# Bias rows moved to GpSimd, expert 2 added in one late pass, and the routing moved behind the last gate

## The chip, the cores and the metric

The kernel runs on one core of one Trainium2 chip. The metric is the time of one execution in microseconds (us); lower is better. TensorE is called PE here, VectorE DVE, ScalarE ACT, GpSimd POOL and the queue that issues the DMAs SP, as in the profile.

## The reference, cut to what matters

The input x has 16 groups of 512 tokens with 128 features each. All weights are small and shared by the groups.

```python
xn  = layernorm(x)
out = x + attn(xn) + ffn(xn)
# attn: queries, keys, values of 32 features; decayed causal scores; 128 features out, times out_scale
# ffn, for every token:
logits  = xn @ router_w + router_b + load_balancer      # 4 experts
rw, sel = top_k(logits, 2); rw = softmax(rw)
e0 = silu(xn @ sw_w1) * (xn @ sw_w3) @ sw_w2            # hidden 512
e1 = gelu(three folded linear maps) @ me_c2w + me_c2b   # hidden 256
e2 = layernorm(h2 + ff(h2)) @ ce_gen_w + ce_gen_b       # h2 itself a layernorm of a linear map of xn
e3 = gelu(xn @ ml_w1 + ml_b1) @ ml_w2 + ml_b2           # hidden 512
ffn = rw[0] * stack(e0, e1, e2, e3)[sel[0]] + rw[1] * stack(e0, e1, e2, e3)[sel[1]]
```

Every expert is computed for every token. Its weight `coef[:, t, e]` is zero where the expert isn't among the two chosen.

## The kernel before

The work goes in 16 turns, one for each group of 512 tokens (four tiles `t` of 128). The function `turns` writes turns 0 and 1, then a loop whose body holds two turns (2 to 13), then turns 14 and 15 and a tail. Each engine has its own list of instructions, written out by hand in the order in which it runs them, and semaphores between them; no scheduler moves anything. A waiting instruction holds up all that stands behind it on its engine.

A turn g works on group g and on what is left of group g-1 (`g.prev()`), and gets group g+1 ready:

- PE multiplies, in this order: the token products `tok0` to `tok3` (they wait for `x_split`, the low half `xl` of the transposed input), q and k, the first gate (`a0`, `b0`), the hidden units of expert 3 (`c0` to `c3`), the transposes of the normalized tile `n1` (they wait tile by tile for `c_normed`), the scores, the second gate, experts 1 and 2 of group g-1 into the banks EX, the attention, the two `f1` units, the last two gates, `e3`, `f2`, `m0` and `m1`. Then expert 0 of group g goes into the bank that expert 2 also uses (`EX_BANK = {3: 0, 0: 1, 2: 1, 1: 0}`), so it waits for `ex_taken[2]`, and last the transposes of `u`.
- DVE builds `pl` (tokens plus logits) and its moments, the gates (`silu(j)`: L818 and L822), the low halves, the routing (ten small steps, L883 to L898 and L918, each of which waits for the one before, `route`), and mixes the experts: `mix` adds `coef * expert` to `OUT` in four instructions, one a tile (L752). Expert 2 is mixed in two passes, `expert2_scale` (L762, expert 2 times its `rstd`, plus its bias) and `expert2_add` (L771). The bias of expert 1 is added by four more (L926). Near the end of the turn stand `u` (L931), `x_low` (L706, the `xl` for which the next turn's first products wait) and `x_moments` for group g+2 (L640, L643).
- ACT takes the products out of PSUM: tanh, gelu, relu, the high halves of the split numbers, and `tlean` (L612), the tanh that turns the difference of two logits into their softmax.
- POOL runs, in every turn: `norm("c")` (L444 to L454: the root of the variance and four tiles of `n1`), `root_u`, six low halves (`hid3l`, `hidl`, L486 and L490), and `norm_x` for group g+2, which waits for `x_moments`. The next thing on its list is the next turn's `norm("c")`, which waits for `c_stats`, the moments of `pl`.
- SP carries the normalized x and the transposed expert 3 to memory and back (`swap`), loads x and stores the output (`store` waits for `out_ready`).

The order on POOL and what `norm("c")` is needed for are in these lines:

```python
# POOL, turn(g)
norm("c", pl, n1, c_normed)
...                               # root_u, hid3l, hidl
norm_x(Group(g.pair, g.off + 2))
# PE, turn(g)
pe.wait_ge(c_normed, g.count(NT, t + 1))
ins = pe.transpose(TR[:, t * P:(t + 1) * P], n1[:, t, :], ident[:, :])
# PE, expert0(g)
wait(pe, ex_taken[2], g.count(1, 0))
```

## Time and profile before

| what | value |
|---|---|
| median of 3 runs | 451.15 us (451.05 to 454.04) |
| span of the profiled execution, first to last instruction | 449.1 us |
| so outside the span, against the median | 2.05 us |
| PE busy | 438.6 us, 98% of the span |
| DVE busy | 402.5 us, 90% |
| ACT busy | 271.4 us, 60% |
| POOL busy | 245.8 us, 55% |
| from one turn to the next | 26.83 us |

The time of the profiled execution as a whole isn't listed beside its span; the medians are taken for it. A turn's length is the distance of the same instruction in two turns: the first transpose of `n1` starts at 207.64 and at 234.48 us. In a row of the timeline the first number is the start in us from the beginning of the span, the second is the duration of the piece (of all its instructions, where xN says that there are several), and a bracket at the end gives the engine's idle time before it and what ended it. Instructions of one engine overlap a little: four mixing instructions of 0.345 us take 1.05 us from the first start to the start of what follows.

### The profile page before, as it was taken

The page shows a single profiled execution, that of the slowest core. Times are in us where ns is not written, and L with a number is a line of the kernel's source. Part 1 is how long each engine was busy: PE and PEld are TensorE (multiplying, and loading weights), DVE is VectorE, ACT ScalarE, POOL GpSimd, SP SyncE. Part 2 cuts the span into 40 slices and gives each one's busy share as a digit, 9 for nine tenths or more (in the row PEclk, how much of TensorE's full clock was granted, in tenths as well). Part 3 has the DMA queues.
Part 4 walks back from the last instruction along what each step waited for, and adds up shares of the span by engine and source line. Part 5 has one row for each costly group of instructions (what it writes and reads, how often), then busy time and mean ns, then how long its engine had stood idle before and what let it go on. Part 6 is the DMA issues. An engine that isn't in the chain of part 4 may idle for free.

```text
span 449.1 us, 9603 instructions
## 1 busy us (share of the span) xinstructions
PE 438.6 (98%) x2804; PEld 371.8 (83%) x2804; DVE 402.5 (90%) x1344; ACT 271.4 (60%) x535; POOL 245.8 (55%) x366
## 2 busy tenths in 40 slices
PE   4999999999999999999999999999999999999997
PEld 3778888788888888888888988888888888888886
DVE  4887989989899898989989899898989989898897
ACT  4965838557384764838556484755838566483841
POOL 3893727557273664727466272664727466372451
PEclk9999999999999999999999999999999999999999
DMA  7522123032130412223032130413123031220201
GB/s 261 38 72 72 25 63 78 26 93 47 51 70 23 105 35 70 47 70 70 23 93 47 55 62 23 113 27 89 27 70 70 23 99 41 58 58 16 58 0 48
DMA packets 86484, 27.18 MB, mean 61 GB/s; under 512 B 64993, under 2 KB 82113, under 8 KB 86465
## 3 DMA queue, kind: packets, MB, share of 16 engines
q1 hardware_dynamic: 86176, 26.94, 25.0%
q8 instruction: 9, 0.15, 0.1%
q14 instruction: 11, 0.08, 0.1%
q10 hardware_dynamic: 288, 0.01, 0.0%
HBM read 14.66 MB, written 12.06 MB: 60 GB/s over the span
## 4 chain that ended last, share of the span: by engine, by line
PE 94%; DVE 3%; DMA 1%; issue 0%; DVEq 0%; ACT 0%; SPq 0%
PE S L1133 14%; PE S L1135 13%; PE S L1134 13%; PE EX L1059 12%; PE EX L1079 6%; PE S L1223 3%; PE S L1218 3%; PE S L1219 3%; PE EX L1087 3%; PE TR L1173 2%; PE S L1231 2%; PE S L1230 2%; PE S L1229 2%; PE S L1148 2%; PE S L1147 2%; PE S L1146 2%
## 5 line engine op out<-in xcount | busy, mean ns | idle before, releaser
L486 POOL TENSOR_TENSOR hid3l<-hid,hid3h 128x512 fp32r<-128x512 f32 x64 | 80.3, 1287 | 29.3 <-ACT hid3h L599 29.3
L1133 PE MATMUL S<-xh,WH 128*128 128x512 f32 x224 | 90.4, 403 | 0.0
L1135 PE MATMUL S<-xh,WL 128*128 128x512 f32 x224 | 88.4, 394 | 0.0
L1134 PE MATMUL S<-xl,WH 128*128 128x512 f32 x224 | 88.1, 393 | 0.0
L444 POOL TENSOR_TENSOR veps_x<-mv_x,eps 128x4 f32<-128x4 f32 x16 | 3.2, 200 | 111.7 <-DVE mv_x L643 111.7
L1059 PEld LDWEIGHTS EX<-scaled,hid 128*128 128x128 f32 x480 | 55.9, 192 | 1.2
L1059 PE MATMUL EX<-scaled,hid 128*128 128x128 f32 x480 | 56.0, 275 | 0.0
L1133 PEld LDWEIGHTS S<-xh,WH 128*128 128x128 f32 x224 | 42.2, 188 | 14.1 <-DVE hid L822 3.1
L1135 PEld LDWEIGHTS S<-xh,WL 128*128 128x128 f32 x224 | 42.1, 188 | 9.9
L573 ACT COPY kv<-S 128x64 f32<-128x64 f32 x64 | 13.6, 213 | 60.3 <-PE S L1148 54.6
L1134 PEld LDWEIGHTS S<-xl,WH 128*128 128x128 f32 x224 | 42.3, 189 | 8.0
L822 DVE TENSOR_TENSOR hid<-gate,S 128x512 f32<-128x512 f32 x64 | 44.0, 688 | 4.2
L490 POOL TENSOR_TENSOR hidl<-hid,hidh 128x512 fp32r<-128x512 f32 x32 | 40.9, 1300 | 11.0 <-ACT hidh L609 11.0
L818 DVE SCALAR_TENSOR_TENSOR gate<-th,S 128x512 f32<-128x512 f32 x64 | 43.8, 684 | 1.8
L567 ACT ACTIVATE th<-S 128x512 f32<-128x512 f32 x64 | 38.1, 595 | 8.8 <-PE S L1135 6.9
L588 ACT ACTIVATE hid<-S,VEC 128x512 f32<-128x512 f32 x64 | 38.8, 690 | 0.4
L752 DVE SCALAR_TENSOR_TENSOR OUT<-EX,coef,OUT 128x128 f32<-128x128 f32 x124 | 34.8, 344 | 0.6 <-PE EX L1069 0.2
L599 ACT CAST hid3h<-hid 128x512 fp32r<-128x512 f32 x64 | 34.6, 615 | 0.0
L621 ACT ACTIVATE hid<-S,me_b 128x512 f32<-128x512 f32 x32 | 22.0, 687 | 19.2 <-PE S L1135 19.1
L519 ACT CAST xh<-TR 128x512 fp32r<-128x512 f32 x16 | 9.4, 588 | 37.6 <-DVE TR L800 37.4
L1079 PEld LDWEIGHTS EX<-W,hid 128*128 128x128 f32 x240 | 29.1, 191 | 1.3
L454 POOL TENSOR_SCALAR n<-pl,negmean_c,rstd_c 128x128 f32<-128x128 f32 x64 | 27.8, 451 | 2.8 <-issue 2.8
(201 smaller groups left out, 1066.4 us busy)
## 6 DMA issues: line engine op xcount, KB each, us to landing
X<-x SPq DMA_DIRECT2D x16, 256.0 KB, 2.8
turning<-xn SPq DMA_DIRECT2D x15, 256.0 KB, 2.6
xb<-turning SPq DMA_DIRECT2D x60, 64.0 KB, 2.6
turning<-e3T SPq DMA_DIRECT2D x15, 256.0 KB, 2.4
e3b<-turning SPq DMA_DIRECT2D x60, 64.0 KB, 2.6
out<-OUT SPq DMA_DIRECT2D x15, 256.0 KB, 2.4
W<-weights SPq DMA_DIRECT2D x1, 768.0 KB, 8.2
W<-weights SPq DMA_DIRECT2D x1, 512.0 KB, 5.8
```

Source lines behind the costliest of these rows:

```text
L486: pool.tensor_tensor(hid3l[:, j, :], hid[3][:, j, :], hid3h[:, j, :], ALU.subtract) \
L490: pool.tensor_tensor(hidl[:, j, :], hid[2][:, j, :], hidh[:, j, :], ALU.subtract) \
L567: act.activation(th[:, j, :], a[:, :], ACT.Tanh, scale=0.5).then_inc(th_ready, 1)
L588: act.activation(hid[3][:, j, :], c[:, :], ACT.Gelu, bias=vec(f"ml_b1{j}")).then_inc(free, 1)
L752: ins = dve.scalar_tensor_tensor(out=OUT[g.par][:, t, :], in0=(src or EX[EX_BANK[e]])[:, t, :], scalar=coef[g.par][:, t, e:e + 1], in1=OUT ...
L818: dve.scalar_tensor_tensor(out=gate[:, j, :], in0=th[:, j, :], scalar=1.0, in1=a[:, :], op0=ALU.add, op1=ALU.mult).then_inc(a_free, 1)
L822: dve.tensor_tensor(hid[0][:, j, :], gate[:, j, :], b[:, :], ALU.mult).then_inc(b_free, 1)
L1059: ins = pe.matmul(EX[EX_BANK[0]][:, t, :], hid[0][:, j, t * P:(t + 1) * P], scaled[:, j * P:(j + 1) * P], start=(j == 0), stop=(j == 3))
L1079: ins = pe.matmul(EX[EX_BANK[1]][:, t, :], hid[1][:, j, t * P:(t + 1) * P], w("me_c2w", j * P, P), start=(j == 0), stop=(j == 1))
L1133: pe.matmul(bank[:, :], wh, hi, start=True, stop=False)
L1134: pe.matmul(bank[:, :], wh, lo, start=False, stop=False)
L1135: pe.matmul(bank[:, :], wl, hi, start=False, stop=True).then_inc(unit_ready, 1)
```

## The change

- The bias of expert 1 (`me_c2b`) and the bias of expert 2 (`gen_bias`) are multiplied with their weights and added to `OUT` by POOL: a new function `add_biases(g)` with four instructions on 128x512 elements and two drains. It waits for `att_added` and for the last step of the routing of group g, and stands between `hidl` and `norm_x`. DVE's four instructions of L926 go.
- Expert 2 of group g-1 is mixed by one pass `expert2` of four instructions straight from its PSUM bank, with `coef * rstd` as the factor, behind the routing. `expert2_scale` and `expert2_add` go.
- The routing's first nine counted steps move from behind the second gate to behind the last gate and `turn_next`, and their scratch from PSUM (`TR`) to SBUF. ACT's `tlean` moves behind `e3T`.
- DVE takes the first gate before the low half of q.
- The turn's end: `coef` now comes before the transpose `e3t`; `store` waits for the mixing of expert 3, which is the last one; the tail loses the four instructions of L949, and `mix(g, 3, ...)` of the last group waits for POOL's sum.

```diff
             # POOL, turn
                     pool.tensor_tensor(hidl[:, j, :], hid[2][:, j, :], hidh[:, j, :], ALU.subtract) \
                         .then_inc(hid_low, 1)
+                add_biases(g, first)
                 if two_more(g):
                     norm_x(Group(g.pair, g.off + 2))
+
+            def add_biases(g, first):
+                if first:
+                    pool.wait_ge(bias_rows_loaded, 2 * DMA_INC)
+                    pool.wait_ge(setup_took, TAKEN.index("gen_b") + 1)
+                pool.wait_ge(att_added, g.count(1, 1))
+                pool.wait_ge(route_step, g.count(ROUTE_STEPS, ROUTE_STEPS))
+                wide = [P, NT, P]
+                pool.tensor_tensor(bias1[:, :, :], row("me_c2b").unsqueeze(1).broadcast_to(wide),
+                                   coef[g.par][:, :, 1:2].broadcast_to(wide), ALU.mult)
+                pool.tensor_tensor(bias2[:, :, :], gen_bias[:, :].unsqueeze(1).broadcast_to(wide),
+                                   coef[g.par][:, :, 2:3].broadcast_to(wide), ALU.mult)
+                pool.drain()
+                pool.tensor_tensor(bias1[:, :, :], bias1[:, :, :], bias2[:, :, :], ALU.add)
+                pool.drain()
+                ins = pool.tensor_tensor(OUT[g.par][:, :, :], OUT[g.par][:, :, :], bias1[:, :, :], ALU.add)
+                ins.then_inc(biases_added, 1)
             # ACT, turn
-                act.wait_ge(lean_ready, g.count(1, 1))
-                act.activation(tlean[:, :, :], lean[:, :, :], ACT.Tanh).then_inc(tlean_ready, 1)
                 half_gate(3)
...
+                act.wait_ge(lean_ready, g.count(1, 1))
+                act.activation(tlean[:, :, :], lean[:, :, :], ACT.Tanh).then_inc(tlean_ready, 1)
                 for j in range(2):
                     m, free = unit(f"m{j}")
             # DVE
-            def expert2_scale(g):
-            def expert2_add(g):
+            def expert2(g):
                 dve.wait_ge(u_rstd, g.count(1, 1))
+                dve.tensor_tensor(coef_r[:, :], coef[g.par][:, :, 2], rstd["u"][:, :], ALU.mult).then_inc(u_scaled, 1)
+                dve.wait_ge(u_scaled, g.count(1, 1))
                 dve.wait_ge(ex_ready[2], g.count(1, 1))
+                dve.wait_ge(ex_taken[1], g.count(1, 1))
+                for t in range(NT):
+                    ins = dve.scalar_tensor_tensor(out=OUT[g.par][:, t, :], in0=EX[EX_BANK[2]][:, t, :],
+                                                   scalar=coef_r[:, t:t + 1], in1=OUT[g.par][:, t, :],
+                                                   op0=ALU.mult, op1=ALU.add)
                 ins.then_inc(ex_taken[2], 1)
...
-                dve.wait_ge(qk_high, g.count(2, 1))
-                dve.tensor_tensor(Q[C:2 * C, :], qk_bank[C:2 * C, :], Q[C:2 * C, :], ALU.subtract)
                 silu(0)
                 if not first:
                     u_combine(g.prev())
+                dve.wait_ge(qk_high, g.count(2, 1))
+                dve.tensor_tensor(Q[C:2 * C, :], qk_bank[C:2 * C, :], Q[C:2 * C, :], ALU.subtract)
...
                 silu(3)
                 if not first and not last:
                     turn_next(g)
+                route(...)        # nine counted steps and lean, as before, scratch in SBUF
+                if first:
+                    turn_next(g)
+                if not first:
+                    expert2(g.prev())
+                dve.wait_ge(tlean_ready, g.count(1, 1))
+                route(...)        # coef
                 if not first:
                     ...           # e3t
-                    mix(g.prev(), 3, ex_taken[1], src=e3t)
+                    mix(g.prev(), 3, ex_taken[2], src=e3t)
```

On POOL, in the loop's body, from the last two low halves of a turn to `norm_x`, the kernel before has these rows, in which `hidl` is the low half for `f2` and `xn` the normalized x of the group after next:

```order
L490 TENSOR_TENSOR hidl<-hid,hidh 128x512 [waits hid_high]
L490 TENSOR_TENSOR hidl<-hid,hidh 128x512
L458 REGISTER_ALU
L444 TENSOR_TENSOR veps_x<-mv_x,eps 128x4 [waits x_stats]
L445 TENSOR_TENSOR negmean_x<-mv_x,minus 128x4
L447 TENSOR_TENSOR rstd_x<-veps_x,nhalf 128x4
L454 TENSOR_SCALAR xn<-X,negmean_x,rstd_x 128x128 x4
L477 REGISTER_ALU
L444 TENSOR_TENSOR veps_c<-mv_c,eps 128x4 [waits c_stats]
L445 TENSOR_TENSOR negmean_c<-mv_c,minus 128x4
L447 TENSOR_TENSOR rstd_c<-veps_c,nhalf 128x4
L454 TENSOR_SCALAR n<-pl,negmean_c,rstd_c 128x128 x4
```

The changed kernel has these in the same place:

```order
L492 TENSOR_TENSOR hidl<-hid,hidh 128x512 [waits hid_high]
L492 TENSOR_TENSOR hidl<-hid,hidh 128x512
L504 ISA [waits att_added]
L506 TENSOR_TENSOR bias<-ROW,coef 128x512 [waits route_step]
L508 TENSOR_TENSOR bias<-gen_bias,coef 128x512
L511 TENSOR_TENSOR bias<-bias 128x512
L513 TENSOR_TENSOR OUT<-OUT,bias 128x512
L460 REGISTER_ALU
L446 TENSOR_TENSOR veps_x<-mv_x,eps 128x4 [waits x_stats]
L447 TENSOR_TENSOR negmean_x<-mv_x,minus 128x4
L449 TENSOR_TENSOR rstd_x<-veps_x,nhalf 128x4
L456 TENSOR_SCALAR xn<-X,negmean_x,rstd_x 128x128 x4
```

Four tensor instructions of the full width and their wait for `route_step` now stand ahead of `norm_x`, and so also ahead of the next turn's `norm("c")`.

On DVE, in the loop's body, from the transpose of expert 3 (`e3t`) to `xl`, the kernel before has these rows, in which `u` is the input of expert 2's last product and `xl` the low half of the next group:

```order
L915 STREAM_TRANSPOSE e3t<-e3b 128x512 [waits e3_swapped,ex_taken3]
L918 SCALAR_TENSOR_TENSOR coef<-tlean,half 128x16 [waits tlean_ready]
L830 REGISTER_ALU
L752 SCALAR_TENSOR_TENSOR OUT<-e3t,coef,OUT 128x128 [waits ex_taken1,ex_ready3,route_step]
L752 SCALAR_TENSOR_TENSOR OUT<-e3t,coef,OUT 128x128 x3
L926 SCALAR_TENSOR_TENSOR OUT<-ROW,coef,OUT 128x128 [waits att_added]
L926 SCALAR_TENSOR_TENSOR OUT<-ROW,coef,OUT 128x128 x3
L805 REGISTER_ALU
L931 SCALAR_TENSOR_TENSOR u<-S,VEC,h 128x512 [waits unit_ready]
L705 REGISTER_ALU
L706 TENSOR_TENSOR xl<-TR,xh 128x512 [waits x_high]
```

In the changed kernel, behind the ten rows of the routing that now follow `TR<-xb`, stand these:

```order
L786 SCALAR_TENSOR_TENSOR OUT<-EX,coef_r,OUT 128x128 [waits ex_taken1,ex_ready2,u_scaled]
L786 SCALAR_TENSOR_TENSOR OUT<-EX,coef_r,OUT 128x128 x3
L924 SCALAR_TENSOR_TENSOR coef<-tlean,half 128x16 [waits tlean_ready]
L844 REGISTER_ALU
L130 REGISTER_ALU [waits route_step]
L929 STREAM_TRANSPOSE e3t<-e3b 128x512 [waits e3_swapped,ex_taken3]
L773 SCALAR_TENSOR_TENSOR OUT<-e3t,coef,OUT 128x128 [waits ex_taken2,ex_ready3]
L773 SCALAR_TENSOR_TENSOR OUT<-e3t,coef,OUT 128x128 x3
L819 REGISTER_ALU
L934 SCALAR_TENSOR_TENSOR u<-S,VEC,h 128x512 [waits unit_ready]
L726 REGISTER_ALU
L727 TENSOR_TENSOR xl<-TR,xh 128x512 [waits x_high]
```

`expert2` now reads the bank of expert 2 here and not some 8 us earlier, `coef` stands behind it, and the routing, `expert2` and `coef` all stand ahead of `u` and `xl`; the four rows of L926 and the four of L771 are gone.

## Rows read from the trace of the kernel before

**Rows 1.** The page: busy time of PE to POOL, granted clock, chain by engine.

```profile
PE 438.6 (98%) x2804; PEld 371.8 (83%) x2804; DVE 402.5 (90%) x1344; ACT 271.4 (60%) x535; POOL 245.8 (55%) x366
...
PEclk9999999999999999999999999999999999999999
...
PE 94%; DVE 3%; DMA 1%; issue 0%; DVEq 0%; ACT 0%; SPq 0%
```

**Rows 2.** Timeline of POOL, turn 7 and start of turn 8.

```profile
211.14 5.03 POOL L486 TENSOR_TENSOR hid3l<-hid,hid3h 128x512 fp32r<-128x512 f32 x4 [1.96 <-ACT hid3h L599]
...
227.25 0.20 POOL L444 TENSOR_TENSOR veps_x<-mv_x,eps 128x4 f32<-128x4 f32 x1 [7.83 <-DVE mv_x L643]
...
228.93 1.74 POOL L454 TENSOR_SCALAR xn<-X,negmean_x,rstd_x 128x128 f32<-128x128 f32 x4 [0.17 <-issue]
231.29 0.20 POOL L444 TENSOR_TENSOR veps_c<-mv_c,eps 128x4 f32<-128x4 f32 x1 [0.63 <-DVE mv_c L853]
...
232.96 1.74 POOL L454 TENSOR_SCALAR n<-pl,negmean_c,rstd_c 128x128 f32<-128x128 f32 x4 [0.18 <-issue]
```

**Rows 3.** Timeline of PE, turn 8: the transposes of `n1`.

```profile
234.48 0.65 PE L1173 MATMUL TR<-ident,n 128*128 128x128 f32 x4
```

**Rows 4.** Timeline of PE's weight loads, end of turn 7: expert 0, `u`, first token product.

```profile
223.68 3.77 PEld L1059 LDWEIGHTS EX<-scaled,hid 128*128 128x128 f32 x32
227.36 0.47 PEld L1246 LDWEIGHTS ATT<-ident,u 128*128 128x128 f32 x4
227.80 0.19 PEld L1146 LDWEIGHTS S<-TH,xh 128*128 128x128 f32 x1
```

**Rows 5.** Timeline of DVE, turn 7: first routing step, `foundl`, what follows the routing.

```profile
213.06 0.17 DVE L883 COPY TR<-pl 128x16 f32<-128x16 f32 x1
...
214.31 0.29 DVE L716 TENSOR_TENSOR foundl<-ATT,foundh 128x128 fp32r<-128x128 f32 x1
...
215.50 1.13 DVE L762 SCALAR_TENSOR_TENSOR e<-EX,rstd_u,gen_bias 128x128 f32<-128x128 f32 x4
```

**Rows 6.** Timeline of DVE, turn 7: from the last gate to the moments of x.

```profile
219.43 0.69 DVE L822 TENSOR_TENSOR hid<-gate,S 128x512 f32<-128x512 f32 x1
...
220.67 0.67 DVE L915 STREAM_TRANSPOSE e3t<-e3b 128x512 f32<-128x512 f32 x1
221.26 0.13 DVE L918 SCALAR_TENSOR_TENSOR coef<-tlean,half 128x16 f32<-128x16 f32 x1
221.44 1.14 DVE L752 SCALAR_TENSOR_TENSOR OUT<-e3t,coef,OUT 128x128 f32<-128x128 f32 x4
...
223.55 0.74 DVE L931 SCALAR_TENSOR_TENSOR u<-S,VEC,h 128x512 f32<-128x512 f32 x1
224.21 0.68 DVE L706 TENSOR_TENSOR xl<-TR,xh 128x512 fp32r<-128x512 f32 x1
...
225.85 0.87 DVE L640 BATCH_NORM_STATS2 stats_x<-X 128x6 f32<-128x128 f32 x4
```

**Rows 7.** Timeline of POOL, start: the low halves of the weights, one by one.

```profile
11.69 2.36 POOL L471 TENSOR_TENSOR WL<-W,WH 128x1024 fp32r<-128x1024 f32 x1 [1.72 <-DVE xn L696]
...
14.01 2.29 POOL L471 TENSOR_TENSOR WL<-W,WH 128x768 fp32r<-128x768 f32 x1
```

**Rows 8.** DVE: timeline at the start, and the tile `h2l` (min/median/max ns).

```profile
13.33 1.27 DVE L710 TENSOR_TENSOR backl<-back,backh 128x512 fp32r<-128x512 f32 x1
...
L875 DVE TENSOR_TENSOR h2l<-h,h2h x16: 678/693/694, 23.1 to 424.8; 128x512 fp32r<-128x512 f32 x16
```

**Rows 9.** POOL: the tile `rstd_u` (min/median/max ns, first and last start).

```profile
L500 POOL TENSOR_TENSOR rstd_u<-veps_u,nhalf x16: 1006/1007/1188, 47.2 to 442.6; 128x4 f32<-128x4 f32 x16
```

**Rows 10.** Timeline of DVE, end of turn 15.

```profile
437.83 0.74 DVE L931 SCALAR_TENSOR_TENSOR u<-S,VEC,h 128x512 f32<-128x512 f32 x1
```

**Rows 11.** Timeline of PE, end of turn 15: the transposes of `u`.

```profile
438.69 0.60 PE L1246 MATMUL ATT<-ident,u 128*128 128x128 f32 x4
```

**Rows 12.** Waits: engine and line, for whom; us in total, times, longest.

```profile
PEld S L1133 <- DVE gate L818: 3.1, 15, 0.2
```

More of the change, by code:

```diff
@@ L202, in build @@
         rstd = {k: sb(f"rstd_{k}", [P, NT]) for k in "xcu"}
-        more = sb("more", [P, NT, E, E])
+        same, more = (sb(name, [P, NT, E, E]) for name in ("same", "more"))
+        again, rank, top = (sb(name, [P, NT, E]) for name in ("again", "rank", "top"))
+        topsum = sb("topsum", [P, NT])
         lean = sb("lean", [P, NT, E])
@@ L832, in turn @@
                 logit = pl[:, :, P:P + E]
[L833 to L837 removed]
+                mine = again[:, :, :].unsqueeze(3).broadcast_to([P, NT, E, E])
                 other = logit.unsqueeze(2).broadcast_to([P, NT, E, E])
@@ L911, in turn @@
                     turn_next(g)
+                route(dve.tensor_copy(again[:, :, :], logit))
+                route(dve.tensor_tensor(same[:, :, :, :], other, mine, ALU.is_equal))
+                route(dve.tensor_tensor(same[:, :, :, :], same[:, :, :, :],
+                                        earlier[:, :, :].unsqueeze(1).broadcast_to([P, NT, E, E]), ALU.mult))
+                route(dve.tensor_tensor(more[:, :, :, :], other, mine, ALU.is_gt))
+                route(dve.tensor_tensor(same[:, :, :, :], more[:, :, :, :], same[:, :, :, :], ALU.add))
+                route(dve.tensor_reduce(rank[:, :, :], same[:, :, :, :], AX.X, ALU.add))
+                route(dve.scalar_tensor_tensor(out=top[:, :, :], in0=rank[:, :, :], scalar=1.5, in1=logit,
+                                               op0=ALU.is_lt, op1=ALU.mult))
+                route(dve.tensor_reduce(topsum[:, :], top[:, :, :], AX.X, ALU.add))
+                dve.scalar_tensor_tensor(out=lean[:, :, :], in0=topsum[:, :].unsqueeze(2).broadcast_to([P, NT, E]),
+                                         scalar=-0.5, in1=logit, op0=ALU.mult, op1=ALU.add).then_inc(lean_ready, 1)
+                route(dve.tensor_scalar(half[:, :, :], rank[:, :, :], 1.5, 0.5, ALU.is_lt, ALU.mult))
+                if first:
[3 more added lines that the diff above has]
+                dve.wait_ge(tlean_ready, g.count(1, 1))
+                route(dve.scalar_tensor_tensor(out=coef[g.par][:, :, :], in0=tlean[:, :, :], scalar=1.0,
+                                               in1=half[:, :, :], op0=ALU.add, op1=ALU.mult))
                 if not first:
@@ L916, in turn @@
                         .then_inc(ex_ready[3], 1)
-                dve.wait_ge(tlean_ready, g.count(1, 1))
-                route(dve.scalar_tensor_tensor(out=coef[g.par][:, :, :], in0=tlean[:, :, :], scalar=1.0,
-                                               in1=half[:, :, :], op0=ALU.add, op1=ALU.mult))
-                if first:
-                    turn_next(g)
-                if not first:
-                    mix(g.prev(), 3, ex_taken[1], src=e3t)
-                dve.wait_ge(att_added, g.count(1, 1))
-                for t in range(NT):
-                    ins = dve.scalar_tensor_tensor(out=OUT[g.par][:, t, :], in0=row("me_c2b"),
-                                                   scalar=coef[g.par][:, t, 1:2], in1=OUT[g.par][:, t, :],
-                                                   op0=ALU.mult, op1=ALU.add)
-                ins.then_inc(bias1_added, 1)
+                if not first:
+                    mix(g.prev(), 3, ex_taken[2], src=e3t)
                 f2, free = unit("f2")
@@ L934, in turn @@
                     x_low(g.next())
-                if not first:
-                    expert2_add(g.prev())
                 if two_more(g):
```

63 lines of the change are left out of this document (13 added, 50 removed).

## The prediction

> **What bounds the kernel now.** Start with the page [rows 1]: PE is busy for 98% of the span and the chain that ended last runs through PE for 94% of it. PE has no idle time to give back, so nothing that is taken off DVE or POOL shortens a turn unless PE waits for it. The question is therefore only what PE waits for, now and afterwards. Next come the timelines of one turn of 26.83 us, here from turn 7 to turn 8, engine by engine. Read in each the last moment at which PE needs something. There are four such moments: the first weight load of expert 0 at 223.68, that of `u`'s transposes at 227.36, that of the token products at 227.80 [rows 4], and the fourth transpose of `n1`, which starts some 0.4 us behind the first, so near 234.87 (four in 0.65 us [rows 3]). Then read when the other engines deliver. DVE has `u` by 224.21 and `xl` by 224.89 [rows 6], 3 us early. POOL is the tight one. It idles for 7.83 us until the moments of x arrive, runs `norm_x` from 227.25 to 230.67 (3.42 us), waits 0.63 us more, and runs `norm("c")` from 231.29 to 234.70 [rows 2]. PE's fourth transpose comes 0.17 us after that. So POOL's 55% of busy time hides that its last step ahead of PE has hardly any slack: whatever starts `norm("c")` later by more than some 0.1 us is paid by PE in every turn.
>
> **The change part by part**, in the clock of turn 7. Up to the last gate DVE is paced by PE and ACT, so the last gate still ends at 219.43 + 0.69 = 220.12 [rows 6]. The time that the routing leaves free behind the second gate turns into idle time.
>
> *Routing, later.* In the old place it took from 213.06 to 215.50, less some 0.24 for the `foundl` in its midst: 2.2 us for ten steps, 0.22 each [rows 5]. Scratch in SBUF may save a little of it; I take 2.2. It starts where the transpose of expert 3 stood, at 220.67 [rows 6], and ends at 222.87.
>
> *Expert 2 in one pass.* The factor and its wait cost about one routing step, 0.25, then four mixing instructions cost 1.05 (from 221.44 to 223.55 DVE did eight, 2.11 [rows 6]). It ends at 224.2. PE wants its bank at 223.68 [rows 4]: a wait of 0.6 us that wasn't there.
>
> *Coef* is 0.18 (221.26 to 221.44 [rows 6]), so POOL can start at 224.37. Before, DVE had `coef` at 221.4.
>
> *The biases on POOL.* POOL has run 128x512 subtractions four at a time in 5.03, so 1.26 each [rows 2]. Four make 5.0, two drains of about 0.17 (the idle in front of `xn` [rows 2] follows one) make it 5.35. The broadcast operands are not in the trace; I bound an instruction by 1.18 (2.36 for 1024 elements) and 1.53 us (2.29 for 768 [rows 7]), and take 1.26, the row of the same size. Without any disturbance the biases end at 229.72, `norm_x` at 233.14, and `norm("c")` starts at 233.17 in place of 231.29: 1.9 us late, and PE with it. DVE's eight saved instructions (L926 and one of expert 2's passes, 2.1 us a turn) buy nothing, as DVE wasn't what PE waited for.
>
> *POOL and DVE at the same time.* In a turn of before, DVE's mixing of expert 3 (both inputs in SBUF) runs while POOL idles. Now it falls into the bias instructions. The start of the trace shows what that costs. `backl`, a DVE subtraction of two SBUF tensors, took 1.27 us, the same form as `h2l` only 0.69 [rows 8]. It began at 13.33 while POOL's instruction ran from 11.69 to 14.05, and it ended at 14.60, that is 0.55 after POOL's end. POOL's next one started at 14.01 and took 2.29 for 768 elements, while 1024 took 2.36 [rows 7]: it seems to have waited for `backl`. So the two took turns, and each waited for the whole of the other's instruction. In the tail POOL's `rstd_u`, 1.007 us as a rule, took 1.188 at 442.6 [rows 9], where DVE ran four such mixing instructions in a row: it waited for one of them, not for all four. I take it that POOL gets in between DVE's instructions, and DVE between POOL's.
>
> Then: the first bias instruction runs from 224.37 to 225.63, and the first mixing instruction waits for its end. The second bias instruction gets in next, 225.75 to 227.0. Behind it POOL drains, and two mixing instructions pass. The third runs 227.35 to 228.6, then the last mixing instruction. So `u` starts at 228.85 in place of 223.55, `xl` ends 1.34 later, at 230.2. PE's token products wait for it: 2.45 late. The moments of x start at 230.1 and take 1.3, `norm_x` starts at 231.5 and takes 3.42, `norm("c")` starts at 234.9 in place of 231.29: 3.6 late. That is the turn's price, since the waits before it are inside it and the rest of the turn hangs on PE from there.
>
> *The Trainium skill* bears on this. Its page "SBUF — State Buffer", section "Who interferes with whom", says that DVE and GpSimd share one pair of ports under an exclusive lock, that a DVE instruction with two SBUF inputs contends with a GpSimd instruction that reads SBUF, and that the second to issue is blocked until the first has finished. By that rule the mixing of expert 3 is blocked here, while the plain sum gives 1.9 us a turn and not 3.6. `backl` agrees (1.27 against 0.69 us [rows 8]). That page gives no order for two queues of such instructions.
>
> *The first gate ahead of q's low half* frees its banks earlier. PE's weight loads waited there for 3.1 us over 15 turns [rows 12], for each of the gate's two instructions. They run ahead of the products, so at most that comes back, and now PE stands waiting a little later for `norm("c")` anyway: nothing.
>
> *Store, tlean.* `store` is 3 us later, with DMAs needed again only 20 us later; `tlean` runs at 222.8 beside expert 2's pass: nothing.
>
> *The tail.* In turn 15 `u` is late by the same 5.3 us (437.83 in before [rows 10]), PE had 0.2 us to spare (438.69 [rows 11]), and all that ends the kernel hangs on it: 5.1 us. The four removed instructions of L949 don't help, since the last mixing of expert 3 waits for the biases too.
>
> *Sum.* Fourteen boundaries between turns (0 to 14) have `norm_x` in them: 14 x 3.6 = 50.4. The boundary from 14 to 15 has none, there `xl` decides: 2.4. Tail: 5.1. Together 57.9, on the span of 449.1, or on the median of 451.15: **509 us**.
>
> **The rivals.**
>
> *The biases and DVE don't disturb each other.* Then a turn costs 1.9, the last boundary 0.6 (expert 2's bank), the tail 4.2 (the biases' end): 26.6 + 4.8 = 31.4, so 482.5 us. `backl` speaks against it.
>
> *DVE keeps the ports for its four instructions in a row.* One wait only; mixing ends at 226.7, POOL's biases at 230.75, `norm("c")` starts 2.9 late: 40.6 + 0.6 + 5.2, so 497.5 us. The `rstd_u` row speaks against it.
>
> *Strict turns, one for one.* The drains don't let a second one pass; mixing ends at 230.25, `xl` at 231.6, `norm("c")` starts 5.05 late: 70.7 + 3.9 + 6.6, so 532 us.
>
> *Only expert 2's bank is paid.* If POOL's four instructions took under 3.5 us, 15 x 0.6 = 9: 460 us. Nothing in rows 2 supports that.
>
> *Not slower.* POOL's idle 7.83 us covers the biases and DVE's saved 2.1 us pulls everything forward. The mechanism is DVE's lighter end of turn: it decides if the biases are done by the time the moments of x are, that is if `coef` plus the biases end by 227.3, 3.0 us after `coef` and not 5.35, and expert 2's pass ends by 223.7. Then only PE's waits at the first gate go, of which at most 3.1 us come back [rows 12]; with a third of that, 450 us. The idle time speaks for it; it lies before 224.4, though, and not behind.
>
> *The clock.* It was granted at full level throughout [rows 1]. PE would now stand still for some 2.4 and then 1.2 us a turn; if that took it to the lower level, the time would go beyond 532.
>
> **How the numbers follow.** 509: 0.36. Strict turns, 532: 0.16. One wait, 497.5: 0.15. No disturbance, 482.5: 0.16. Bank only, 460: 0.05. Not slower, 450: 0.05. Clock or worse: 0.07. The range 482 to 533 leaves out the last three, 0.17, and takes in the bounds of the bias instruction (4 x 0.27 x 15 = 16 us up, 5 down). A measurement of this kernel tells about 1%. Faster by more: 0.02; within it: 0.04; slower by more: 0.94.
>
> **What would show it.** A turn of some 30.4 us; PE idle before the transposes of `n1` with POOL's n1 named, and before the token products or `u`'s transposes with DVE named; the mixing of expert 3 from `e3t` with a mean well above 0.35 us; POOL's idle before `veps_c` gone; DVE idle before L897 and L832. I am wrong if PE's first wait is at expert 0's load alone, if the mixing keeps its 0.345 us, or if the bias instructions take far from 1.26 us.

## The result and the profile after

The changed kernel takes **501.91 us** (median of 4 runs, 500.80 to 502.95) where the kernel before, run beside it, took 451.78 (4 runs): 1.1115 times as long, 95% interval 1.1082 to 1.1147. The execution in the trace took 502.95 us with a span of 501.2, against 449.1 before, so 52.1 us are to be found. The page, whose lines answer to [rows 1]:

```profile
PE 462.1 (92%) x2804; PEld 381.9 (76%) x2804; DVE 402.7 (80%) x1231; ACT 272.6 (54%) x535; POOL 321.4 (64%) x430
...
PEclk9999899999999999999999999999999999999998
...
POOL 34%; issue 27%; POOLq 16%; PE 11%; DVE 8%; ACT 2%; DMA 1%; DVEq 0%; SPq 0%
```

PE has fallen from 98% to 92% of a longer span, and the chain that ended last, once 94% PE, goes through POOL and its queue. DVE's busy time is the same as before (402.7 against 402.5) although it has 113 instructions fewer. The groups of instructions say why (line, engine, operation, busy us and mean ns of one, idle time before):

```profile
L506 POOL TENSOR_TENSOR bias<-ROW,coef 128x512 f32<-128x512 f32 x16 | 16.8, 1048 | 78.8 <-DVE coef L924 78.8
...
L773 DVE SCALAR_TENSOR_TENSOR OUT<-e3t,coef,OUT 128x128 f32<-128x128 f32 x60 | 45.7, 819 | 0.5
...
L773 DVE SCALAR_TENSOR_TENSOR OUT<-EX,coef,OUT 128x128 f32<-128x128 f32 x124 | 34.9, 344 | 3.8 <-PE EX L1075 1.5
```

The same instruction of the same line takes 344 ns when its source is EX, in PSUM, and 819 when it is `e3t`, in SBUF. What PE waited for (us in total, times, longest):

```profile
PEld ATT L1241 <- DVE u L934: 18.5, 15, 4.7
...
PEld ATT L1150 <- DVE stats_u L801: 9.9, 13, 1.2
PEld EX L1055 <- DVE OUT L786: 9.0, 14, 1.0
PEld TR L1168 <- POOL n L456: 6.6, 19, 2.0
```

A steady turn, from the timeline of POOL, to be laid beside [rows 2]; the last gate's second instruction on DVE starts at 244.61:

```profile
249.52 1.05 POOL L506 TENSOR_TENSOR bias<-ROW,coef 128x512 f32<-128x512 f32 x1 [4.92 <-DVE coef L924]
250.53 1.09 POOL L508 TENSOR_TENSOR bias<-gen_bias,coef 128x512 f32<-128x512 f32 x1
...
255.88 0.20 POOL L446 TENSOR_TENSOR veps_x<-mv_x,eps 128x4 f32<-128x4 f32 x1 [1.31 <-DVE mv_x L664]
...
259.27 0.20 POOL L446 TENSOR_TENSOR veps_c<-mv_c,eps 128x4 f32<-128x4 f32 x1
```

And DVE's, beside [rows 6]:

```profile
244.61 0.69 DVE L836 TENSOR_TENSOR hid<-gate,S 128x512 f32<-128x512 f32 x1
...
249.28 0.17 DVE L924 SCALAR_TENSOR_TENSOR coef<-tlean,half 128x16 f32<-128x16 f32 x1
...
250.22 3.09 DVE L773 SCALAR_TENSOR_TENSOR OUT<-e3t,coef,OUT 128x128 f32<-128x128 f32 x4
253.24 0.74 DVE L934 SCALAR_TENSOR_TENSOR u<-S,VEC,h 128x512 f32<-128x512 f32 x1
```

Coef starts 4.67 us after that gate instruction starts (before: 221.26 less 219.43, 1.83). The four mixing instructions take 3.09 in place of 1.14. Even so POOL, done with the biases, stands 1.31 us waiting for the moments of x; `norm_x` starts late because DVE is late, and `norm("c")` starts right behind it (14.66 us after the gate instruction, 11.86 before). That is 2.80 us, and it is the turn: expert 0's first weight load comes every 29.6 us (101.20 to 397.42 in ten turns), before every 26.83.

Where the 52.1 us are, from those loads: 3.7 in the first turn, of which 3.0 stand ahead of its first gate (20.63 us, before 17.66); 5.1 at the boundary from turn 0 to 1; 36.4 in thirteen boundaries of 2.8; 6.9 from there to the end. The first turn varies by up to 3 us from one profiled execution to another (first load at 39.53 here, at 37.38 in e3 and at 36.38 in e1 below, whose first turns are the same code up to there), so I compare turns wherever I can.

### The profile page after: what moved, and what is told of

The parts are those of the page before. It is cut to its first block, busy times and chain, and to the rows that moved or that the text cites. A ratio compares the mean times of both kernels' runs of the same rounds, so it can differ in the third digit from the quotient of the medians.

```text
span 501.2 us, 9588 instructions
## 1 busy us (share of the span) xinstructions
PE 462.1 (92%) x2804; PEld 381.9 (76%) x2804; DVE 402.7 (80%) x1231; ACT 272.6 (54%) x535; POOL 321.4 (64%) x430
## 3 DMA queue, kind: packets, MB, share of 16 engines
HBM read 14.66 MB, written 12.06 MB: 53 GB/s over the span
## 4 chain that ended last, share of the span: by engine, by line
POOL 34%; issue 27%; POOLq 16%; PE 11%; DVE 8%; ACT 2%; DMA 1%; DVEq 0%; SPq 0%
POOL hid3l L488 10%; POOL hidl L492 6%; POOLq L454 6%; POOLq L512 4%; POOL n L456 4%; POOL OUT L513 4%; POOL xn L456 3%; POOLq L510 3%; POOL bias L508 3%; POOL rstd_u L521 2%; POOLq L448 2%; DVE gate L832 1%; DVE OUT L773 1%; POOLq L520 1%; PE EX L1075 1%
## 5 line engine op out<-in xcount | busy, mean ns | idle before, releaser
L506 POOL TENSOR_TENSOR bias<-ROW,coef 128x512 f32<-128x512 f32 x16 | 16.8, 1048 | 78.8 <-DVE coef L924 78.8
L1055 PEld LDWEIGHTS EX<-scaled,hid 128*128 128x128 f32 x480 | 54.8, 192 | 9.1 <-DVE OUT L786 9.0
L832 DVE SCALAR_TENSOR_TENSOR gate<-th,S 128x512 f32<-128x512 f32 x64 | 43.8, 684 | 20.8 <-ACT th L588 20.8
L1055 PE MATMUL EX<-scaled,hid 128*128 128x128 f32 x480 | 57.5, 278 | 2.9 <-DVE OUT L786 2.9
L773 DVE SCALAR_TENSOR_TENSOR OUT<-e3t,coef,OUT 128x128 f32<-128x128 f32 x60 | 45.7, 819 | 0.5
L897 DVE TENSOR_TENSOR OUT<-ATT,X 128x512 f32<-128x512 f32 x16 | 11.1, 692 | 27.3 <-PE ATT L1204 27.3
```

The source lines that it names most:

```text
L773: ins = dve.scalar_tensor_tensor(out=OUT[g.par][:, t, :], in0=(src or EX[EX_BANK[e]])[:, t, :], scalar=coef[g.par][:, t, e:e + 1], in1=OUT ...
L832: dve.scalar_tensor_tensor(out=gate[:, j, :], in0=th[:, j, :], scalar=1.0, in1=a[:, :], op0=ALU.add, op1=ALU.mult).then_inc(a_free, 1)
L1055: ins = pe.matmul(EX[EX_BANK[0]][:, t, :], hid[0][:, j, t * P:(t + 1) * P], scaled[:, j * P:(j + 1) * P], start=(j == 0), stop=(j == 3))
```

## The experiments

Turns are the distance between expert 0's first weight loads, averaged over nine or more turns. The kernel before has 26.83 us, the changed one 29.62.

**e1. The changed kernel without the bias work.** Left out are the four wide instructions and the drains; the bias rows are never added.

```diff
-                pool.tensor_tensor(bias1..., row("me_c2b")..., coef[...1:2]..., ALU.mult)
...
-                ins = pool.tensor_tensor(OUT[g.par]..., OUT[g.par]..., bias1..., ALU.add)
+                ins = pool.tensor_tensor(touched[:, :], eps4[:, :], eps4[:, :], ALU.add)
```

> The changed kernel with the four wide bias instructions and their drains on GpSimd left out (the bias rows are never added; a 128x4 addition waits and signals in their place), all else as in the changed kernel: late routing, one late pass of expert 2. My theory, that the 2.8 us a turn come from GpSimd's bias work (its 5.1 us in front of norm("x"), and the blocking of the mixing of expert 3), expects a turn of 26.8 to 27.4 us and 455 to 463 us, the rest being the turns 0 and 15 and PE's wait for expert 2's bank. The rival, that the late routing (2.2 us between the last gate and x_moments) carries the loss by itself, expects about 2 us a turn kept, 480 us or more.

Measured: 467.22 us, ratio 1.037 [1.0334, 1.0407], turn 27.77. The mixing from `e3t` is back at 1.14 us for four. So the bias work costs 1.85 us a turn in this surrounding, and 0.94 is there without it, more than I had allowed. PE pays 0.6 of it in every turn before expert 2's bank, and the rest in some turns before `stats_u` (five waits, 1.7 us together), in the others before `n1`. A turn of the first kind:

```profile
230.97 3.65 PEld L1048 LDWEIGHTS EX<-scaled,hid 128*128 128x128 f32 x32 [0.61 <-DVE OUT L779]
...
236.69 0.19 PEld L1143 LDWEIGHTS ATT<-xh,WH 128*128 128x128 f32 x1 [0.29 <-DVE stats_u L794]
```

**e2. POOL just as busy, but reading nothing.** Memsets of nearly the same length; the bias rows are never added.

```diff
-                pool.tensor_tensor(bias1..., row("me_c2b")..., coef[...1:2]..., ALU.mult)
+                pool.memset(filler[:, 0:1116], 0.0)
...
-                ins = pool.tensor_tensor(OUT[g.par]..., OUT[g.par]..., bias1..., ALU.add)
+                pool.memset(filler[:, 0:1300], 0.0)
```

> The changed kernel with the four bias instructions replaced by memsets of about the same length (1116, 1116, 1349 and 1300 elements a partition by the rate of the two memsets of the setup rows, 0.84 ns an element, and two 128x4 additions, 4.9 us together) that write SBUF and read nothing; the bias rows are never added. If GpSimd's reads of SBUF block VectorE's two-SBUF-source mixing, the mixing is free here and only the queue in front of norm("x") stays: GpSimd would be done near 254.6 where norm("x") started at 255.9 in the changed kernel, so 1.3 us a turn come back and 1.5 stay: 480 to 486 us, the mixing instructions at 0.35 us. If the loss were the occupation of GpSimd alone, with no blocking, nothing comes back: 499 to 503 us.

Measured: 478.36 us, ratio 1.062 [1.0571, 1.067], turn 28.1, just under my range. POOL of e2:

```profile
238.59 1.03 POOL L507 MEMSET filler<- 128x1116 f32 x1
239.55 1.03 POOL L508 MEMSET filler<- 128x1116 f32 x1
240.70 1.22 POOL L510 MEMSET filler<- 128x1349 f32 x1
242.04 1.18 POOL L512 MEMSET filler<- 128x1300 f32 x1
243.34 0.20 POOL L447 TENSOR_TENSOR veps_x<-mv_x,eps 128x4 f32<-128x4 f32 x1
```

The mixing from `e3t` takes 348 ns on average, beside memsets of nearly the same length. The wait for `mv_x` is gone, and POOL's queue alone decides. Of the 1.85 us of the bias work, 0.35 is its place in POOL's queue, and 1.5 is that it reads SBUF while DVE mixes from SBUF. The Trainium skill has this distinction ("SBUF — State Buffer", section "SBUF: two separate sides"): a DVE instruction with two SBUF inputs needs the shared ports only against a GpSimd instruction that reads SBUF. The trace agrees: 348 ns beside memsets, 819 beside the bias instructions.

**e3. Expert 3 mixed behind the moments of x.** In every turn but the last:

```diff
-                if not first:
+                if last:
                     wait(dve, ex_taken[3], g.prev().count(1, 0))
                     ... (transpose e3t, mix expert 3)
...
                 if two_more(g):
                     x_moments(Group(g.pair, g.off + 2))
+                if not first and not last:
+                    ... (transpose e3t, mix expert 3)
```

> The changed kernel with expert 3's transpose and its mixing moved behind u, x_low and x_moments in every turn but the last (nothing left out). The bias work and its contention stay, but the moments of x no longer stand behind the blocked mixing. Blocking theory: mv_x is there before GpSimd has done the biases, norm("x") starts when they end, 1.3 us earlier than in the changed kernel: 28.3 us a turn, 480 to 487 us. Rival, that GpSimd's queue alone decides when norm("x") starts: no gain, 500 us or more.

Measured: 484.34 us, ratio 1.0713 [1.0675, 1.0751], turn 28.4. The biases stay as they were and 1.2 us a turn come back from DVE's order alone. Blocking costs where the blocked instruction stands ahead of what sets the turn. Here that is POOL's queue: from the first bias instruction (240.21) to the end of `norm("c")` (252.19) POOL waits for no other engine. The mixing is still blocked (mean 621 ns), and PE waits 0.97 us in most turns for `stats_u`, which now stands right behind it; but `mv_c` is there before POOL gets to it, so that this wait doesn't lengthen the turn.

**e4. The routing back in its old place.** Its scratch stays in SBUF.

```diff
                 if first:
                     found_rest(g)
+                route(dve.tensor_copy(again[:, :, :], logit))
+                ... (the routing, as in the changed kernel)
-                route(dve.tensor_copy(again[:, :, :], logit))
-                ... (the same lines, behind the last gate)
```

> The changed kernel with the routing instructions (VectorE) and the tanh (ScalarE) back in their old places, their scratch still in SBUF; biases on GpSimd and the single pass of expert 2 stay. The coefficients are ready 2.2 us earlier after the last gate, and the bias work and the blocked mixing begin that much earlier. I expect norm("c") 12.5 us after the last gate (14.66 in the changed kernel, 11.86 before), so about 0.6 us a turn of the 2.8 stay: 455 to 465 us. Rival, that the blocked mixing costs the same wherever the routing stands: 27.5 us a turn or more, at least 480 us.

Measured: **520.07 us**, ratio 1.1529 [1.1505, 1.1554], turn 30.7. Both of my readings missed: it is slower than the changed kernel, and not through the mixing, which takes its 3.1 us as there. In the timeline of DVE, beside [rows 5]:

```profile
246.66 0.38 DVE L893 COPY again<-pl 128x16 f32<-128x16 f32 x1
247.07 1.26 DVE L894 TENSOR_TENSOR same<-pl,again 128x64 f32<-128x64 f32 x1
248.37 1.20 DVE L895 TENSOR_TENSOR same<-same,earlier 128x64 f32<-128x64 f32 x1
249.59 0.22 DVE L897 TENSOR_TENSOR more<-pl,again 128x64 f32<-128x64 f32 x1
...
250.57 1.27 DVE L903 SCALAR_TENSOR_TENSOR top<-rank,pl 128x16 f32<-128x16 f32 x1
251.87 0.17 DVE L905 TENSOR_REDUCE topsum<-top 128x4 f32<-128x16 f32 x1
252.07 1.01 DVE L906 SCALAR_TENSOR_TENSOR lean<-topsum,pl 128x16 f32<-128x16 f32 x1
```

The POOL rows of the same stretch:

```profile
244.50 4.98 POOL L488 TENSOR_TENSOR hid3l<-hid,hid3h 128x512 fp32r<-128x512 f32 x4 [1.62 <-ACT hid3h L620]
250.52 2.53 POOL L492 TENSOR_TENSOR hidl<-hid,hidh 128x512 fp32r<-128x512 f32 x2 [1.04 <-ACT hidh L630]
```

An instruction on 64 elements takes 1.26 us in place of 0.23. Each one that has both operands in SBUF ends when one of POOL's six subtractions ends (248.3, 249.5, 251.8, 253.05); `more`, which falls in POOL's pause from 249.5 to 250.5, takes 0.22; `topsum`, a reduction with one source, runs through beside `hidl` in 0.17. The routing takes 6.5 us in place of 2.4. In the kernel before the scratch was TR, in PSUM, so only one operand came from SBUF. The two edits of the routing belong together: with its scratch in SBUF it can't stand where POOL subtracts.

**e5. e4 with the scratch in PSUM.**

```diff
+                same = TR[:, 0:NT * E * E].rearrange(...)
+                again, rank, top = (TR[:, (E + n) * NT * E:...] for n in range(3))
```

> The changed kernel with routing and tanh in their old places and the routing's scratch in TR, a PSUM bank, as before; biases on GpSimd and the late single pass of expert 2 stay. It differs from e4_route_early in the place of the scratch (and one found_rest step). New theory, read in the trace of e4_route_early: with scratch in SBUF, routing instructions that take both operands from SBUF are blocked by GpSimd's hid3l subtractions, which run at that time, 6.5 us for the routing in place of 2.4. With PSUM scratch the routing is back at 2.4 us, the coefficients come 2.2 us earlier than in the changed kernel, GpSimd ends its bias work near 7.2 us after the last gate, and about 0.7 us a turn remain from the blocked mixing: 458 to 466 us. Rival, that an early routing with biases on GpSimd is slow wherever its scratch lies: above 505 us.

Measured: 462.53 us, ratio 1.0232 [1.0199, 1.0265], turn 27.41. The place of the scratch is worth 57.5 us between e4 and e5. With the routing early, the whole bias work on POOL and the late pass of expert 2 together cost 0.6 us a turn, though the mixing is blocked as much as ever (3.09 us).

**e6. The kernel before, its scratch in SBUF, and nothing else.**

```diff
-                same = TR[:, 0:NT * E * E].rearrange(...)
+        same, more = (sb(name, [P, NT, E, E]) for name in ("same", "more"))
```

> The kernel before with one thing changed: the routing's scratch tiles in SBUF in place of TR, at the same place in the program. Theory: the routing falls on GpSimd's hid3l (211 to 216 us in the trace of before) and is blocked for about 4.1 us a turn on VectorE, foundl comes 2.4 us late for TensorE: about 3 us a turn, 485 to 500 us. Rival, that e4_route_early was slow for its biases and not for its scratch: 450 to 456 us.

Measured: **517.76 us**, ratio 1.1479 [1.144, 1.1518], turn 30.76; I had 485 to 500. DVE is as late as I thought, and PE waits 2.52 us for `foundl`. What I hadn't counted is behind that wait. The windows of 2 us (busy time of PE, PEld, DVE, ACT, POOL; granted clock; DMA share; GB/s):

```profile
246.00:248.00 2.00, 0.08 (x1) 0.08 (x1) 1.89 (x5) 1.61 (x2) 1.22 (x2) 1.00 0.00 0
248.00:250.00 2.00, 2.00 (x7) 1.57 (x8) 1.90 (x3) 0.00 (x0) 2.00 (x2) 0.71 0.00 0
250.00:252.00 2.00, 2.00 (x6) 1.53 (x5) 1.96 (x7) 0.70 (x2) 0.24 (x1) 0.50 0.00 0
252.00:254.00 2.00, 2.00 (x9) 1.64 (x8) 1.97 (x4) 0.60 (x1) 0.00 (x0) 0.93 0.24 73
```

PE comes back at the lower level (0.50 of 2.4 GHz is 1.2) and has 7, 6 and 9 matmuls in these windows, where the one behind them, at 1.00, has 10. Those three windows lack 0.29 + 0.50 + 0.07 of 2 us each, 1.7 us, beside the 2.5 of the wait.

**e7. e5 with expert 2's pass ahead of the gates.**

```diff
-                if not first:
-                    expert2(g.prev())                    (behind the last gate)
...
+                if not first:
+                    expert2(g.prev())                    (ahead of OUT<-ATT,X)
```

> As e5_route_early_in_psum, with the single pass of expert 2 moved ahead of the gates too (where its scaling stood before), so that only the bias rows on GpSimd and the saved pass are left of the change. The coefficients come 1.2 us earlier again, mv_x with them; norm("x") would start near 7.3 us after the last gate as before (7.13), GpSimd's bias work being then the last to end. I expect 0 to 0.3 us a turn: 450 to 456 us. Rival, that 5 us on GpSimd cost over 1 us a turn wherever they stand: above 465 us.

Measured: 457.92 us, ratio 1.0144 [1.0114, 1.0174], turn 27.20. Over my range. The 0.37 us a turn are PE's wait of 0.54 for the second gate (L1218 for L831). Ahead of that gate stands the little product `coef_r`, here in the tile view (min/median/max ns):

```profile
L779 DVE TENSOR_TENSOR coef_r<-coef,rstd_u x15: 164/676/691, 55.1 to 436.3; 128x4 f32<-128x4 f32 x15
```

and the same view of e5, where it stands behind the gates:

```profile
L779 DVE TENSOR_TENSOR coef_r<-coef,rstd_u x15: 144/147/155, 60.3 to 443.0; 128x4 f32<-128x4 f32 x15
```

Four elements a partition, and it waits for half of a POOL subtraction. That this is what makes the second gate late is read from the rows; no run moves `coef_r` alone.

**e8. The kernel before with only the first gate ahead of q's low half.**

```diff
-                dve.wait_ge(qk_high, g.count(2, 1))
-                dve.tensor_tensor(Q[C:2 * C, :], ...)
                 silu(0)
                 if not first:
                     u_combine(g.prev())
+                dve.wait_ge(qk_high, g.count(2, 1))
+                dve.tensor_tensor(Q[C:2 * C, :], ...)
```

> The kernel before with only the first gate put ahead of q's low half. VectorE has room there and TensorE is what is late, so nothing: 449 to 453 us, at most 1 us gained. Rival: the gate releases ScalarE and GpSimd 0.7 us earlier each turn and TensorE follows, up to 0.3 us a turn: 446 us; or K, Q come 0.7 us late for TensorE: 455 us or more.

Measured: 452.21 us, ratio 1.0025 [1.0007, 1.0044], turn 26.81. The waits of [rows 12] are gone from the view and nothing is gained; this part of the change is neutral.

**e9. e7 with expert 3 mixed last**, as in e3 (same diff, on e7).

> As e7_route_psum_expert2_early (routing early with PSUM scratch, expert 2 early, biases on GpSimd), with expert 3's transpose and mixing behind x_moments in every turn but the last. The 0.4 us a turn that e7 still lost were mv_x late behind the blocked mixing (GpSimd waited 1.30 us for it after its bias work). With the mixing out of that path norm("x") starts when the bias work ends, 7.1 us after the last gate or a little later: 0 to 0.2 us a turn, 450 to 454 us. If it beat the kernel before it would have to go below 449 us, for which nothing speaks, since TensorE is busy all the time in both. Rival, that the loss is GpSimd's occupation: 457 us or more, as e7.

Measured: 458.71 us, ratio 1.0166 [1.013, 1.0202], turn 27.21. Missed. The moments of x are early now and POOL waits 1.66 us for the moments of c, but the turn is that of e7: PE still waits 0.57 us for the second gate. So neither POOL's occupation nor the blocked mixing held e7. What is left is the wait for the second gate, and of what stands ahead of that gate only `coef_r` takes longer than unblocked (0.68 us for 0.15). e12 below takes it away from there, though with the whole pass.

**e10. The kernel before with only the routing moved late**, scratch in SBUF (diff as in the change: the routing lines and the tanh go behind the last gate).

> The kernel before with only the routing (and the tanh) moved behind the last gate, scratch in SBUF; biases on VectorE and expert 2 in two passes as before, the first turn's turn_next ahead of the coefficients. On VectorE 2.2 us now stand between the last gate and x_moments, mv_x is 2.2 us late, norm("x") with it, and norm("c"), which has 0.63 us to spare, about 1.6 us late: 470 to 478 us. Rival, taken from e1_no_bias_work, where the late routing together with the late pass of expert 2 cost 0.95 us a turn with no bias work anywhere: at most 1 us a turn, 465 us or less.

Measured: **507.12 us**, ratio 1.1215 [1.1168, 1.1261], turn 30.76. Both readings missed by far. DVE and PE of e10:

```profile
248.95 0.17 DVE L916 SCALAR_TENSOR_TENSOR coef<-tlean,half 128x16 f32<-128x16 f32 x1 [0.94 <-ACT tlean L620]
```

```profile
256.17 0.29 PEld L1150 LDWEIGHTS ATT<-xh,WH 128*128 128x128 f32 x1 [1.90 <-DVE stats_u L788]
```

The tanh stands behind `e3T` on ACT, which here still waits for DVE's transpose `e3t`: another 0.94 us for DVE. And PE, after 1.90 us of standing, is granted 0.51 and 0.64:

```profile
254.00:256.00 2.00, 0.44 (x4) 0.26 (x3) 1.71 (x11) 0.44 (x3) 0.78 (x3) 1.00 0.51 151
256.00:258.00 2.00, 1.83 (x4) 1.49 (x5) 1.93 (x13) 0.15 (x1) 1.82 (x4) 0.51 0.28 111
258.00:260.00 2.00, 2.00 (x7) 1.58 (x6) 1.07 (x5) 1.28 (x3) 1.83 (x5) 0.64 0.44 69
```

**e11. e10 with the change's wait on ACT.**

```diff
-                wait(act, ex_ready[3], g.count(1, 0))
+                wait(act, e3_kept, g.count(DMA_INC, 0))
```

> As e10_route_late_only, with one more line of the change: ScalarE waits for e3_kept in place of ex_ready[3], so that e3T and the tanh behind it no longer stand behind VectorE's transpose e3t. In e10 VectorE waited 0.94 us for the tanh each turn, TensorE stood idle 1.90 us at L1150 (for stats_u) and was then granted 0.51 and 0.64 for about 4 us, at 30.9 us a turn. Theory: the late routing by itself costs about 2 us of lateness, the tanh's wait another, and the third microsecond or so is the clock that falls after the long wait. Here the wait at L1150 should be about 1 us, as in the changed kernel (0.97, where the clock stayed at 1.00), no lower clock follows, and the turn takes 28.3 to 29 us: 472 to 484 us. Rival, that the order of VectorE's work alone costs 4 us a turn: still above 500 us.

Measured: 477.35 us, ratio 1.0566 [1.0525, 1.0606], turn 28.69. One line is worth 30 us. The wait at L1150 lies between 1.10 and 1.75 us, turn by turn. Behind the one at 246.91 the clock stays:

```profile
246.91 0.19 PEld L1150 LDWEIGHTS ATT<-xh,WH 128*128 128x128 f32 x1 [1.47 <-DVE stats_u L788]
```

```profile
246.00:248.00 2.00, 1.09 (x5) 0.92 (x6) 2.00 (x11) 0.10 (x1) 1.68 (x5) 1.00 0.67 227
```

Behind the one of 1.75 us, at 131.46, it is granted 0.50 from 132 to 134, and that turn takes 30.12 us where those beside it take 28.7 and 28.6. One more thing shows here: with the routing late, DVE's load matters. e11 keeps the bias rows and both passes of expert 2 on DVE and loses 1.86 us a turn; e1, where they are gone, loses 0.94. The two differ in several lines, so this is a hint and not a measurement of the eight instructions.

**e12. The parts put together.** e5, with the coefficients ahead of expert 2's pass and expert 3 mixed last.

```diff
+                dve.wait_ge(tlean_ready, g.count(1, 1))
+                route(dve.scalar_tensor_tensor(out=coef..., ...))
                 if not first:
                     expert2(g.prev())
-                dve.wait_ge(tlean_ready, g.count(1, 1))
-                route(dve.scalar_tensor_tensor(out=coef..., ...))
...                  (expert 3 behind x_moments, as in e3)
```

> Routing early with PSUM scratch as before, biases on GpSimd, and behind the last gate: the coefficients first, then the single pass of expert 2, u, x_low, x_moments, and expert 3's transpose and mixing last. In e7 and e9 TensorE waited 0.54 to 0.57 us a turn for the second gate, which stood behind coef_r (0.67 us in place of 0.16, blocked by hidl); here nothing new stands ahead of the gates, and no two-source instruction stands in front of x_moments while GpSimd works but x_low and expert 2's passes, of which the latter read PSUM. Expected 26.8 to 27.0 us a turn, 450 to 454 us; faster than before by 1% or more is not expected, since TensorE is busy 98% of the time there. Rival, that another wait of half a microsecond turns up: 457 us or more.

Measured: 452.87 us, ratio 1.0039 [1.0014, 1.0064], turn 26.81. The page:

```profile
PE 440.8 (98%) x2804; PEld 376.5 (83%) x2804; DVE 375.0 (83%) x1231; ACT 270.3 (60%) x535; POOL 321.1 (71%) x430
```

All of POOL's bias work is there and costs nothing in a turn: `norm("c")` even waits 1.94 us for its input again. DVE has been relieved by 27.5 us (402.5 to 375.0), and that buys nothing either, as PE is the bound at 98%. The 1.7 us of the medians lie outside the steady turns. The two traces are 3.0 us apart. From the last first load of expert 0 to the end it takes 38.86 us in place of 37.57: in turn 15 expert 3 is still mixed ahead of `u`, its four instructions take 2.19 us beside POOL's, and PE waits 1.30 us for `u`. These 1.3 us are a price of e12's own. The rest is the first turn (first load at 37.80, before at 35.85); e5, whose first turn is the same code, has it at 36.38, so that part varies by execution. No version beat the kernel before.

## Why the prediction was right, and where its sizes were off

**What bounds the kernel.** Right: PE had nothing to give back (e12, with DVE at 83%, is no faster), and what starts `norm("c")` later is paid in every turn: 2.80 us later by the timeline, 2.79 by the turn. The place where PE pays is only in part the one that I named. I had 2.4 us before the token products and the rest before `n1`. In a steady turn PE waits 0.6 us for expert 2's bank, 1.0 for `u`, 0.6 to 1.0 for `stats_u`, which I didn't have, and 0.06 to 0.5 for `n1`. DVE's moments of `pl` are there only 0.2 us before POOL asks for them (259.06, 259.27), so the two paths end almost together. DVE's idle time before L897 and L832 came as forecast (27.3 and 20.8 us in all).

**Routing, expert 2, coef.** Right to a tenth: 2.2 us of routing (245.85 to 248.04), 0.62 of PE's wait at expert 0's load, coef started 4.67 us after the gate instruction where the sum had 4.74 (224.37 less 0.2 for coef itself, less 219.43).

**The bias instructions.** Mis-sized: 1.05 and 1.09 us for the two with broadcast operands, where I took the 1.26 of a plain 128x512 row. With 1.39 and 1.28 for the other two and the drains, 5.06 in place of 5.35. The lower bound of 1.18 was too high as well.

**DVE and POOL take turns.** The mechanism is shown. Reads are what matters (e2: memsets leave the mixing at 348 ns and give back 1.5 us a turn), and the mixing's place ahead of the moments is what makes most of it a price (e3: 1.2 us back). The pattern of three waits came as forecast. For one turn, the tile views of the mixing and of the biases (min/median/max ns):

```profile
L773 DVE SCALAR_TENSOR_TENSOR OUT<-e3t,coef,OUT x4: 339/745/1351, 220.8 to 222.4; 128x128 f32<-128x128 f32 x4
```

```profile
L511 POOL TENSOR_TENSOR bias<-bias x1: 1392/1392/1392, 222.2 to 222.2; 128x512 f32<-128x512 f32 x1
```

One mixing instruction passes in 0.34 us, one takes 1.35, the time of the POOL instruction that it met, and L511 itself is 0.12 longer than L513 where it met one of DVE's. **The term of the sum that was mis-sized is this one, 3.6 us a turn.** I had mixing start at 225.1 and `u` at 228.85, 3.75 later; it took 3.02 (250.22 to 253.24). The order of the waits was right. The rows of that turn show where the 0.73 are: the first two bias instructions were 0.2 each shorter than I took, POOL's second one started without the gap of 0.12 that I had put there, its drain and the step behind the last wait took 0.14 and 0.08 where I had 0.35 and 0.25, and against that L511 was 0.14 longer. 3.6 less 0.73 is 2.9, against 2.8 measured.

**Sum.** Thirteen boundaries at 2.8 in place of 3.6 are 10.4 us too many in the forecast. The boundary 14 to 15 was put at 2.4 and cost 1.2. The tail was put at 5.1 and took 5.7: `u` was 4.4 late, and what stands behind it took another 1.3, at the lower clock (below). The boundary 0 to 1 cost 5.1 in place of 3.6, also with a lower clock. The rest, some 3.7, is the start, which I hadn't counted. Together: 57.9 forecast, 52.1 in the traces, 509 against 501.9 us. Some of that nearness is luck: the start and the first boundary, 5.2 us that were not in the sum, make up for half of what the thirteen boundaries were put too high.

**The rivals.** *No disturbance* (482.5) is what e2 comes to: 478.4, from the same mechanism, POOL's queue. *Only expert 2's bank* (460) is near e1, 467.2: the bank's 0.6 us is there, and another 0.3 at `stats_u` or `n1` that I hadn't given it. *Strict turns* didn't come: a drain does let a second one pass. *Not slower* fails as said: POOL's idle time lies ahead of `coef`. *The clock* stayed at 1.00 in the steady turns, where PE waits 0.62, 0.96 and 0.97 us at three places; it was nearer than its chance of 0.07 says, since e10, with one wait of 1.6 to 1.9 us, falls into it each turn, and e4, with one of 2.25 to 2.5, in eight of fourteen.

**What I had not seen.** I costed the new home of the scratch at nothing ("may save a little of it"). In its new place that is right, since POOL is idle then. But it is also what forces the routing to be there: at the old place the same scratch costs 66.6 us (e6). And the parts don't add. In turns, against 26.83: late routing with the late pass 0.94 (e1), the biases and the late pass with an early routing 0.58 (e5), all together 2.79. With the routing early `coef` is there sooner: POOL idles 2.72 us ahead of the biases in e5, 4.92 in the changed kernel.

## What to carry to other kernels

Before work goes to GpSimd, list what VectorE runs at that time with both operands in SBUF, above all tiny instructions: each can wait for a whole instruction of GpSimd's, in e4 1.27 us for one worth 0.18. With the scratch in PSUM and the routing early the same bias work cost at most 0.6 us a turn (e5); with, besides, an order on VectorE in which nothing critical stands behind the blocked ones it cost nothing in a steady turn (e12). Where an engine is the bound at 98%, relieving the others gives nothing; what an edit can do there is make it wait, and waits of 1.6 us and more were here often, not always, paid a second time in clock.

## What the runs showed of the hardware

- The blocking goes by the place of the operands and not by size. The product of 128x4 took 676 ns in place of 147 (e7, e5), 128x64 took 1190 to 1268 in place of 225 where it met POOL's subtractions (e6). Reductions with one source ran through (0.17 to 0.22 us beside POOL's subtractions). The plain copy `again<-pl` from SBUF to SBUF, one source, was blocked too: 648 ns on average in e6, 159 in the changed kernel, and the one at 243.87 ended at 244.49, when the second of POOL's subtractions from 241.96 on did. The section "SBUF: two separate sides" of the Trainium skill's page "SBUF — State Buffer" lets a fast two-port mode of DVE take the shared ports too, and names the fp32 copy from SBUF to SBUF as what runs in it. The rows agree in that the copy waits; in which mode it ran, no run here shows.
- It goes both ways: in e9 POOL's `rstd_x`, beside DVE's mixing, took 1.20 us in place of 1.02.
- TensorE's granted clock fell to 1.2 GHz behind waits of 1.6 to 1.9 us (e10, every turn), 1.75 (e11, one turn), 1.99 (changed kernel, boundary 0 to 1), 2.5 (e6, every turn) and 4.74 us (the changed kernel's tail), and stayed at 2.4 GHz behind those of 0.97, 1.18 and 1.47. The length of the wait doesn't decide alone. In e4 PE waits 2.25 to 2.50 us for `foundl` in each of fourteen turns, and the clock fell in eight of them; behind this one it stayed at 1.00:

```profile
189.06 0.19 PEld L1202 LDWEIGHTS ATT<-backh,foundh 128*128 128x128 f32 x1 [2.25 <-DVE foundl L737]
```

- What the lower level costs beside the wait: the eight turns of e4 with a fall took 31.1 us on average and the six without 30.1, so 1.0 us; the tail of the changed kernel took 1.3 us longer behind `u`; in three windows of e6 1.7 us of full clock are missing. e10 and e11 are 2.06 us a turn apart, and so 30 us in all. 0.94 of it is the wait for the tanh; the other 1.1 is what a fall cost in e4, an estimate, as no run separates the two.
